# A decoder layer on one core: the last batch's stage by halves of its tiles, first expert weights and last tiles loaded within attention, the two passes of 128 rows done together, tables loaded ahead

## What is computed

```
x = LN(x + attention(x))          # 16 heads of 64, softmax, output projection Wp
# the memory update adds, row by row: 38 rows of conv_b, compressed old rows,
# rows of x moved by a fixed distance, and 154 rows of ctx
x = LN(ctx-memory(ctx, x) + x)
# top-1 routing to 8 experts, 128 rows for each expert of each sequence
logits = x @ Wg; gate = max softmax; expert = argmax; position by a running count
h = gelu(rows[e] @ W1[e])         # 256 -> 1024, tanh form
x = LN(x + gate * (h @ W2[e]))    # 1024 -> 256; tokens past capacity get 0
```

## Time and profile before

| | us |
|---|---|
| median of 3 runs (1963.28 to 1965.1) | 1964.49 |
| the profiled execution | 1964.73 |
| its span, first to last instruction | 1963.0 |
| attention block ends (barrier) | 1669.2 |
| PE busy in the span | 1864.4 (95%) |
| mean granted clock of PE | 0.974 |

### The profile page before, as it was taken

One profiled execution on the slowest core, in us unless ns is written; L12 is line 12 of the kernel. 1 busy time (PEld: TensorE's weight loads), 2 busy tenths in 40 slices (PEclk: granted clock), 3 DMA queues, 4 the chain that ended last, 5 costly groups with the idle time before them and its releaser, 6 DMA issues. The chain is left out here.

```text
span 1963.0 us, 30772 instructions
## 1 busy us (share of the span) xinstructions
PE 1864.4 (95%) x11400; PEld 1189.5 (61%) x11400; DVE 1221.1 (62%) x2145; ACT 864.0 (44%) x1118; POOL 1352.3 (69%) x727
## 2 busy tenths in 40 slices
PE   7899999999999999899999999899999989788996
PEld 5555555556665565556665555566665644688886
DVE  5565666666666667566666577566666677444553
ACT  3343444444344543343454443343445433446663
POOL 1688778787668776886678677885787776444553
PEclk9999999999999999999999999999999999887998
DMA  4300000012211000122111000122110102622330
GB/s 145 89 23 17 23 17 22 23 44 88 75 43 40 17 23 17 36 73 87 44 51 31 17 23 28 44 66 64 43 40 18 33 12 81 188 90 86 122 108 33
DMA packets 134223, 104.25 MB, mean 53 GB/s; under 512 B 58172, under 2 KB 120764, under 8 KB 133052
## 3 DMA queue, kind: packets, MB, share of 16 engines
q1 hardware_dynamic: 131004, 93.81, 16.2%
q0 software_dynamic: 3072, 8.46, 1.2%
HBM read 69.15 MB, written 29.43 MB: 50 GB/s over the span
## 5 line engine op out<-in xcount | busy, mean ns | idle before, releaser
L955 POOL TENSOR_TENSOR prob_sum<-prob_sum,probs 128x1024 f32<-128x1024 f32 (+1 forms) x384 | 906.1, 2360 | 206.9 <-ACT probs L1171 175.0
L1227 DVE TENSOR_REDUCE max_of<-spare_ps 128x1 f32<-128x512 f32 x1024 | 656.8, 683 | 347.7 <-PE spare_ps L1050 337.3
L1171 ACT ACTIVATE probs<-score_ps 128x1024 f32<-128x1024 f32 x512 | 502.4, 1025 | 697.8 <-PE score_ps L1071 697.4
L1085 PE MATMUL av_ps<-probs,v 128*64 128x512 f32 x2048 | 488.0, 602 | 3.0 <-ACT probs L1171 1.6
L1085 PEld LDWEIGHTS av_ps<-probs,v 128*64 128x64 f32 x2048 | 129.8, 136 | 241.1 <-issue 220.3
L951 POOL TENSOR_TENSOR prob_sum<-probs 128x1024 f32<-128x1024 f32 (+1 forms) x64 | 150.4, 2349 | 149.1 <-ACT probs L1171 149.0
L1050 PE MATMUL spare_ps<-k_hi,q_hi 64*128 64x512 f32 x1024 | 231.0, 445 | 21.6 <-DVE max_of L1227 20.8
L1050 PEld LDWEIGHTS spare_ps<-k_hi,q_hi 64*128 64x128 f32 x1024 | 98.9, 185 | 227.2 <-issue 190.5
L1071 PE MATMUL score_ps<-q_hi,k_hi 64*128 64x512 f32 x1024 | 211.4, 408 | 1.1 <-DVE o_in L1277 0.9
L1071 PE MATMUL score_ps<-q_hi,k_lo 64*128 64x512 f32 x1024 | 204.7, 395 | 0.0
L1071 PE MATMUL score_ps<-q_lo,k_hi 64*128 64x512 f32 x1024 | 203.8, 393 | 0.0
(11 more groups left out here) (224 smaller groups left out, 2396.9 us busy)
## 6 DMA issues: line engine op xcount, KB each, us to landing
o_transposed<-o_out SPq DMA_DIRECT2D x64, 256.0 KB, 2.1
w_raw<-in_L_ffn_W_dram SPq DMA_DIRECT2D x16, 1024.0 KB, 5.7
o_in<-o_transposed SPq DMA_DIRECT2D x28, 512.0 KB, 4.1
w_raw<-in_L_attn_Wq_dram SPq DMA_DIRECT2D x64, 64.0 KB, 2.3
w_raw<-in_L_attn_Wk_dram SPq DMA_DIRECT2D x64, 64.0 KB, 2.2
wv_raw<-in_L_attn_Wv_dram SPq DMA_DIRECT2D x32, 128.0 KB, 2.8
shift_rows<-neg_rows SPq DMA_DIRECT2D x256, 1.0 KB
x<-in_x_dram SPq DMA_DIRECT2D x4, 1024.0 KB, 5.8
```

What stands on the lines that cost most here:

```text
L955: pool.tensor_tensor(out, out, probs[:, n % RING, heads], ALU.add).then_inc(prob_added, 1)
L1085: last = pe.matmul(av_ps[hd * E:(hd + 1) * E, :], v[:, quad % 2, kt, 2 * first_head + hd, :], probs[:, n % RING, hd, :], start=(kt == 0), ...
L1171: act.activation(probs[:, n % RING], score_ps[n % 2][:, :, :], ACT.Exp).then_inc(probs_ready, 1)
L1227: dve.tensor_reduce(max_of[:, u % 2, kh, j, hd:hd + 1], bank[:, :], AX.X, ALU.max).then_inc(pass_read, 1)
```

## The change

In the attention block SP now also loads W1[0] (five halves before the end), and at its end, behind waits for the stores, the last products and the last sums, tiles 4 to 7 and W2[0]. The places are buffers of attention (`probs`, `v`), which are now made ahead of both blocks; the raw weights of all experts lie in `v`, and xe, y and h_act in `probs`.

In the tail the first norm runs by halves (tiles 0 to 3, 4 to 7), and so does `move`, with a semaphore for each half and the load of the conv weights between. Old rows and their compression use the bank of the row transposes, and the transposes of pass 1 therefore wait for `comp_added`. Pass 0 has six banks for its chunks, and its `down` is cut in three, with the transposes of x2, the logits and the count between.

The late passes are one group: one transpose step, `up` of both in a row into four banks (`up_late`), gelu on four chunks at once (`gelu_half`), the transposes of the next group, then both `down`s. ACT splits the weights of experts 2 and 3 and W2[2] behind that, ahead of the gelu of pass 4. `load_table` runs an activation of one column, so that the table is loaded there. The last pass computes tiles 0 and 1 ahead of 2 and 3 in `down`, and each tile is added, normed and sent by itself.

```diff
-    def move(self, sp, b):
+    def move(self, sp, b, parts=(0, 1, 2, 3)):
...
-                         ).then_inc(self.moved, 16)
+                         ).then_inc(self.moved if b < self.B - 1 else self.half_moved[part // 2], 16)
...
+    def load_table(self, act, function):
+        act.activation(self.table[:, :], self.eps[:, :], function)
...
+                if h == HALVES - 5:
+                    sp.wait_ge(av_ready, KT * (UNITS - 4))
+                    weights.load(sp, 0, 0)
...
+            sp.wait_ge(av_ready, KT * UNITS)
+            sp.wait_ge(sum_ready, UNITS)
+            for t in range(route.KEPT, TILES):
+                route.load_o(sp, LAST_TILES + t)
+            weights.load(sp, 1, 0)
...
+    GROUPS = [(0,), (1,), (2, 3)] + [(p,) for p in range(WHOLE, len(PASSES))]
...
-            for t in range(route.KEPT, TB):
-                route.load_o(sp, T0 + t)
-                if t in (5, 7):
-                    weights.load(sp, (t - 5) // 2, 0)
             sp.wait_ge(route.sent, 16 * TB * (B - 1))
+            route.load_new(sp, b)
             load_xe(0, 0, B - 1, xe_early_in[0])
-            route.load_new(sp, b)
+            weights.load(sp, 0, 1)
+            sp.wait_ge(route.x1_low_done, 2)
+            sp.wait_ge(route.x1_done, T0 + 2)
+            route.move(sp, b, (0, 1))
             route.load_cw(sp, b)
+            sp.wait_ge(route.x1_low_done, 4)
+            sp.wait_ge(route.x1_done, T0 + 4)
+            route.move(sp, b, (2, 3))
             load_xe(1, 0, B - 1, xe_early_in[1])
-            weights.load(sp, 0, 1)
-            sp.wait_ge(route.x1_low_done, HT)
-            route.move(sp, b)
             weights.load(sp, 1, 1)
             weights.load(sp, 0, 2)
-            weights.load(sp, 1, 2)
             sp.wait_ge(late_sent, 16 * TB)
             for e in range(EARLY):
                 load_xe(e, B - 1, RT, xe_in[e])
             load_xe(EARLY, 0, RT, xe_in[EARLY])
+            weights.load(sp, 1, 2)
...
+            def up_late(p):
+                rows = rows_of(p)
...
+                for c in range(HC):
+                    cols = slice(c % HALF * P, (c % HALF + 1) * P)
...
+                    if c % HALF == HALF - 1:
+                        last.then_inc(h_ready, HALF)
...
             transpose_rows(LATE)
-            pe.wait_ge(route.counts_out, b + 1)
-            for p in range(LATE, len(PASSES)):
+            for p in range(LATE, WHOLE):
+                up_late(p)
+            transpose_rows(LATE + 1)
+            for p in range(LATE, WHOLE):
+                down_begins(p)
+                for i in range(2):
+                    down(p, [B - 1], range(HALF * i, HALF * (i + 1)))
+            for p in range(WHOLE, END):
                 up(p, range(HC))
-                if p + 1 < len(PASSES):
-                    transpose_rows(p + 1)
-                down(p)
+                if p > WHOLE:
+                    transpose_rows(group_of(p + 1))
+                down_begins(p)
+                down(p, range(RT), range(LAST))
+                if p == WHOLE:
+                    transpose_rows(group_of(p + 1))
+                down(p, range(RT), range(LAST, HC))
+            up(END, range(HC))
+            down_begins(END)
+            down(END, [0, 1], range(LAST))
+            down(END, [0, 1], range(LAST, HC))
+            down(END, [2, 3], range(HC))
...
-            for p in range(LATE, len(PASSES)):
+            for p in range(LATE, WHOLE):
+                for i in range(2):
+                    gelu_half(p, i)
+            rows_high(LATE + 1)
+            split_w1(2)
+            split_w1(3)
+            take_root(1)
+            split_w2(2)
+            route.load_table(act, ACT.Gelu_apprx_tanh)
+            for p in range(WHOLE, END + 1):
                 for c in range(HC):
                     gelu(p, c)
...
+                if p == WHOLE:
+                    take_root(LATE)
+                    take_root(LATE + 1)
...
+                if p < END:
+                    route.load_table(act, ACT.Gelu_apprx_tanh)
+            for t in range(RT):
+                take_root(END, slice(t, t + 1))
```

More of the change, by code:

```diff
@@ L145, in __init__ @@
         self.moved = sem("moved")
+        self.half_moved = [sem(f"half_moved{i}") for i in range(2)]
         self.old_ready = sem("old_ready")
@@ L172, with place_last_tiles, add_splits @@
     KEPT = 4
[L174 to L179, removed]
+    SPLITS = 4
+    def place_last_tiles(self, slots):
+        self.o_more = [slot.rearrange("p (c n) -> p c n", n=P) for slot in slots[:self.TB - self.KEPT]]
+    def add_splits(self, pair):
+        self.splits = [part.rearrange("p (i c) r -> p i (c r)", i=self.SPLITS)
+                       .rearrange("p i (c n) -> p i c n", n=P) for part in pair]
         self.x2T_all = self.x1[:, :, :].rearrange("p t (k n) -> p t k n", n=P)
@@ L1389, in __init__, with add_parts, part @@
         self.split = [ctx.enter_context(nc.semaphore(f"w{i + 1}_split")) for i in range(2)]
+    def add_parts(self, nc, ctx, second_high, second_low):
+        def part(name, shape):
+            return self.flat(ctx.enter_context(nc.sbuf_tensor(name, shape, F32R)))
+        first, second = self.shapes
+        self.high = [[part("w1_hi", first), self.flat(second_high)], [part(f"w2_hi{i}", second) for i in range(2)]]
+        self.low = [[part("w1_lo", first), self.flat(second_low)], [part(f"w2_lo{i}", second) for i in range(2)]]
     def flat(self, w):
@@ new lines, in down @@
+            def down(p, tiles, chunks):
+                w = weights.parts(1, PASSES[p][0])
+                pe.wait_ge(h_done, HC * p + chunks[-1] + 1)
+                for t in tiles:
+                    row = (FIRST_ROW[p] + t - PASSES[p][1]) * P
+                    for c in chunks:
+                        for i, (x, y) in enumerate(products):
+                            last = pe.matmul(y_place(p, t)[:, :], h[x][:, c, row:row + P], w[y][:, c, :],
+                                             start=(c == 0 and i == 0), stop=(c == LAST and i == 2))
+                    if chunks[-1] == LAST:
+                        last.then_inc(y_ready, 1)
@@ L1717, in _ @@
                 gelu(0, c)
+            route.load_table(act, ACT.Sqrt)
             split_w1(1)
-            for c in range(2, 5):
-                gelu(0, c)
             route.take_root(act, 1, b)
-            route.norm2(act, b, range(HT))
+            route.norm2(act, b, range(HT, TB))
             for g in range(TB // 2):
                 route.x2T_out(act, b, g, x2T_bank[g])
-            for c in range(5, 7):
+            rows_high(1)
+            for c in range(6, HC):
                 gelu(0, c)
@@ L1727, in _ @@
             route.exp_gates(act, b)
-            gelu(0, LAST)
-            rows_high(1)
-            for j in range(weights.PIECES):
-                split_w2(1, j)
+            split_w2(1)
+            route.load_table(act, ACT.Gelu_apprx_tanh)
             for c in range(HC):
@@ L1769, in add_rows, with norm @@
                     dve.wait_ge(stats_done, TILES_TO[p] + t - t0 + 1)
                     dve.bn_aggr(moments[:, e % 2, t, :], stats[:, e % 2, t, :]).then_inc(moments_done, 1)
-            def norm(p):
+            def norm(p, tiles=None):
                 e, t0, t1 = PASSES[p]
-                dve.wait_ge(root_done, p + 1)
-                dve.reciprocal(scale[:, e % 2, t0:t1], root[:, e % 2, t0:t1]).then_inc(scale_done, 1)
-                dve.wait_ge(scale_done, p + 1)
-                for t in range(t0, t1):
+                tiles = tiles or slice(t0, t1)
+                done = p + 1 + tiles.start - t0
+                dve.wait_ge(root_done, done)
+                dve.reciprocal(scale[:, e % 2, tiles], root[:, e % 2, tiles]).then_inc(scale_done, 1)
+                dve.wait_ge(scale_done, done)
+                for t in range(tiles.start, tiles.stop):
```

484 lines of the change are left out of this document (281 added, 203 removed).

## The result

| | before | changed |
|---|---|---|
| median of 14 runs each, us | 1963.88 | 1970.34 |
| all runs, us | 1961.0 to 1968.0 | 1968.4 to 1971.3 |
| profiled execution, us | 1964.73 | 1970.0 |
| its span, us | 1963.0 | 1968.0 |

What follows compares the result with a forecast made beforehand. PE was taken as busy in whole passes, with first-stage waits and low clock and a 14.5 us end to cut. Gains of 12.4 early, all and 3.2 more given back, then 5.6 less 2.7 and a 9.4 end: 1960 us, range 1949 to 1969.

Steps and rivals of the forecast that it cites:

- Part 1: Block end to the late rows' transposes: ends at 1749.0 against 1761.4, 12.4 us less.
- rival C: Second half's move lands some 7 us later behind the conv weights on SP, delaying pass 1's transposes: 1970; chance 0.12.
- The tile loads' price of 3.8: At the block end, SP's pushes of four tiles and W2[0] hold the barrier until 1673.0, costing 3.8 us.
- Part 2: Late passes to the start of pass 4: starts at 1781.0, 32.0 us against 31.8 before, no gain.
- Part 3: Pass 4 to pass 5, before 30.9 us: pass 5 starts at 1827.3 against 1824.1, giving back the 12.4 and 3.2 more.
- the wait of 10.8 us for the first gelu: In pass 4 after two chunks, PE waits while ACT stands behind W1[3]'s landing and copies; bounds zero and 14 us.
- Part 4: Passes 5 to 9, before 124.4 us: 5.6 less for gelu waits, 2.7 more for the clock, end at 1948.8.
- the 5.6: Passes 5 to 9: `load_table` under the end of `down` removes five gelu waits of 1.1 us, 5.6 us saved.
- Part 5: The end behind the last product: 9.4 us against 14.5, end at 1958.2.
- "Faster": Whole kernel measured below 1960.6 us, chance 0.58.
- a sum of 4.8 us: Whole kernel: span 1958.2 against 1963.0, 4.8 us less than the profiled execution's 1964.73, giving 1959.9.
- Rival A: Late passes' 96 products run at the upper clock level, saving 10.3 us: 1950; chance 0.15.

Runs made afterwards that it cites:

- the table experiments: Gelu table loads added to the kernel before: 1962.12 us, ratio 0.9985; table loads taken from the changed kernel: 1972.51 us, ratio 1.0042.
- sends_behind_splits: Changed kernel with POOL's three sends of pass 1 behind its splits of W1[3] and W2[2]: 1962.49 us, ratio 0.9989 to the kernel before.
- w1_one_pass_later: Changed kernel with W1[e] split one pass later on ACT and POOL: 1944.78 us, ratio 0.9894 to the kernel before.
- w2_first: Changed kernel with W2[2] split ahead of W1[3] on ACT and POOL: 1967.00 us, ratio 1.0007 to the kernel before.
- splits_behind_sends: Kernel without the computation: POOL's eight subtractions beside DVE's, with indirect sends ahead in some stages; DVE's first instruction right behind sends waits 8.96 us.

## Why the prediction was wrong

The direction was wrong and the time lay 1.3 us above the range. By the prediction's steps, with what the trace shows:

- Part 1 was right: pushes to 1673.0, measured 1673.3, first product behind the barrier 1673.8; transposes of the late rows 1749.0, measured 1750.7. The 2.2 us behind `comp_added` were forecast as 2.5, so rival C did not happen; that the result is the 1970 of rival C is chance. The tile loads' price of 3.8 was 4.1 at the barrier, 2.2 to 3.8 net.
- Part 2 was right: pass 4 at 1781.0, measured 1781.95 (part 1 had been 1.7 late), the late products at 1.2 GHz.
- Part 3: the wait of 10.8 us for the first gelu was 11.1. Wrong was the sentence behind it, "Then 36 chunk products 8.75 and 2.5 for the clock after the pause: 1806.0". They ended at 1815.2. 1.3 us came from before, 5.5 from h_lo, which POOL's run behind its sends held for 10.25 us, and the other 2.4 from the second stretch at the lower clock, 12 products from 1806.9 at a granted clock of 0.50, that stood behind this wait. What follows hangs on the last gelu: the load of expert 3's rows was issued at 1821.42, not 1814.9. It would have been 3 us later, but the step from POOL's send to this load took 2.6 us, not 5.66: an error that helped. W1[4] took 6.7 us to land, not 5.3. Pass 5 began at 1835.1, 7.8 us late.
- Part 4: 123.4 us against 121.5; 1.7 of the difference are the waits for rows, the part of the 5.6 that the table experiments find given back.
- Part 5: 9.5 against 9.4.

7.8 + 1.9 + 0.1 are the 9.8 us between 1958.2 and 1968.0. The step that failed is thus the run of pass 4 behind its first gelu: the overlap of POOL's splits with DVE's h_lo was priced at nothing, and it cost a wait of 5.5 us and 2.4 of clock. sends_behind_splits, in which it is gone, measures 1962.5, inside the forecast's own range of 1955 to 1966. In the trace of before the two meet as well (POOL's splits run from 1796.42 to 1801.89), but take turns there:

```profile
1799.09 3.34 DVE L1520 TENSOR_TENSOR h_lo<-h_act,h_hi 128x512 fp32r<-128x512 f32 x2 [0.18 <-ACT h_act L1683]
```

There POOL's run did not stand behind sends. That the two would meet behind a wait that lines them up could be seen from the order of the instructions; the 10 us could not. The Trainium skill ("SBUF — State Buffer", Who interferes with whom) says that a DVE instruction with two SBUF inputs contends with a POOL instruction that reads SBUF. The runs agree, 1.75 us for 0.68. The Trainium skill's same page (SBUF: two separate sides) says that the loser blocks for the other's whole instruction. That fits the turns; where sends stand ahead it falls short, since DVE's one h_lo was kept out for eight of POOL's.

The larger loss, though, was forecast and rightly: the change puts the splits of W1[2] and W1[3] next to each other, so that the single raw buffer's round (POOL's split, load, ACT's copy) lies open ahead of the gelu. w1_one_pass_later, which takes them apart again, is 25.6 us faster: with the wait of 11.1 go 1.6 of the 5.5, 5.5 of the 6.4 ahead of pass 5, and part of what the lower clock cost behind these waits. "Faster" had a chance of 0.58 on a sum of 4.8 us, and one step of that sum, pass 4 behind its first gelu, was off by 7.9. Rival A did not happen in this kernel, at clocks of 0.971 to 0.973 in all 14 runs; but three runs of ten with the loads behind the barrier show it, and every run without the pause.

## What to carry to other kernels

When a stage is made shorter, look at what it covered: a single buffer's round of split, load and copy was hidden by a pass that the change took away. Don't put a run of POOL work right behind its indirect sends if DVE reads two SBUF operands meanwhile, and put a short group of small products behind busy work without a pause. Measure a small term (the barrier, the tables) only in a version in which the clock doesn't jump between runs.

## What the runs showed of the hardware

- An arithmetic run on POOL right behind indirect sends kept DVE's subtraction of two SBUF operands out to its end: 10.25 us for one instruction in the changed kernel, 8.64 in w2_first, 6.21 in w1_one_pass_later (where POOL's run had four pieces), 8.96 in splits_behind_sends. Behind landed sends, or none, they take turns at 1.7 us. Why, no run tells.
- PE stayed at 1.2 GHz for some 20 us without an idle moment on products of 128 columns (changed kernel, clock 0.51 from 1753.7 to 1774.1). It ran the same ones at 2.4 GHz when it came to them with a pause of only 0.35 us (1.00), and in one execution behind a pause of 1.98 us too (1.00).
- The issue of four tile loads of 512 KB on SP took 5.04 us together in the changed kernel, where a single one just ahead (1665.55) took 0.36. What stands behind on SP, the barrier too, waited for the issue and not for the landing: W2[0] was pushed from 1671.57 on and no load of weights in this trace lands in less than 4.9 us, but PE was through the barrier at 1673.8.
